# An LSTM's and an RNN's recurrent sums in two row blocks: twice the matmuls, half the PSUM columns

## The chip, the cores and the metric

One NeuronCore of a Trainium2 chip runs the kernel. The metric is the time of one execution on the device, in microseconds (us); lower is better.

## The reference, cut to what matters

Four sequences (`NB = 4`) of 1024 tokens with 512 features pass through four residual layers. Two of them are recurrent, and they set the order of everything:

```python
# layer 0, an RNN, 1024 steps
next_h = jnp.tanh(xw_t + prev_h @ Wh)                   # h: (4, 512), Wh: (512, 512)
# layer 1: a short convolution, projections, a state-space scan over the tokens
# layer 2, an LSTM, 1024 steps
A = xw_t + prev_h @ Wh                                  # Wh: (512, 2048)
i, f, o = sigmoid(A[:, 0:H]), sigmoid(A[:, H:2*H]), sigmoid(A[:, 2*H:3*H])
g = jnp.tanh(A[:, 3*H:4*H])
next_c = f * prev_c + i * g
next_h = o * jnp.tanh(next_c)
# layer 3: x @ (base_layer + a low-rank matrix of each sequence)
```

Each layer's result is added to its input.

## The kernel before, in words

**Chunks.** The tokens are cut into 32 chunks of 32 steps (`CT`). The layers run as a pipeline over chunks: while chunk i is in the RNN, chunk i-1 is in the state-space layer (`mid`), chunk i-2 in the LSTM and chunk i-3 in the output layer. So chunks 0 and 1 of the program have no LSTM, 2 to 31 have both recurrences, and 32 and 33 have the LSTM alone. Chunks 0 to 3 and 30 to 34 are written out; those between run in a hardware loop (`Fori`, line 246) whose pass holds two chunks. Within a chunk each engine's program goes through the 32 steps in a fixed order, written by hand; the other layers' work stands at certain steps (`SSM_STEP`, `L2_STEP` and others).

**One step on TensorE** (`products`, L968; the RNN's, L1007): first the LSTM's products of half 0 of the gates' columns, then of half 1, then the RNN's, then a few products of the other layers. h is the stationary operand, as two float16 parts: a high part in columns 0 to 3 and the rest in columns 16 to 19 of a tile of 20 (`LO + NB`), the columns between being zero. Wh, also in two float16 parts (`e`), streams. The output columns are spread over the four column tiles `j` of the array (`tile_position=(0, QC * j)`), so that tile j writes PSUM partitions 32j to 32j+19. For the LSTM a product is 128x20 by 128x256; a half has KB = 4 blocks `k`, two parts `e`, four tiles `j`: 32 products; the RNN's are 128x20 by 128x128, 32 of them. A half's first two blocks `k` need h of half 0 (`lstm_h_ready0`), the others h of half 1.

**One step on VectorE**, in order: transpose of the sums of half 0 (L754, 32x32 blocks, PSUM to `lstm_sums`), reduction (L760: the sum from the high part, that from the rest and the input part, which GpSimd has filled in at L344), transpose of half 1, product of gates 0 (L766), output gate (L775), reduction of half 1, new cell 0 (L771), the RNN's transpose (L815), products of gates 1, new h of half 0 (L783) and its two parts (L787, L791), which release TensorE's next step, the same for half 1, and last the RNN's reduction (L821) and the two parts of its h (L857, L859). ScalarE computes the tanh of the gates (L521), of the cell (L526) and of the RNN (L546) between them. GpSimd fills inputs (L344, L358) and runs the state-space layer's series (L371, L372) in certain steps.

**Preparation.** ScalarE converts the RNN's Wh to its high part (L478, four instructions) and VectorE subtracts to get the rest (L673, sixteen); the LSTM's Wh is split in chunk 0. The first step of each recurrence uses the float32 weights (L999, L943).

Of the kernel before, what the change touches and what calls it, by code (L numbers as in the profile page):

```python
# [7 lines left out]
F16 = mybir.dt.float16  # L8
# [6 lines left out]
P = 128  # L15
# [21 lines left out]
XS = 2 * LO  # L37
PIECES = [(0, 14), (14, 24), (24, 30), (30, 32)]
# [55 lines left out]
def resid_stack_kernel(nc, x, cond, l0_Wx, l0_Wh, l0_b, conv_b, Wp, bp, Ws, bs, A_log, dt_log, Wo, bo,  # L94
                       l2_Wx, l2_Wh, l2_b, base, w1, b1, w2, b2, ln_g, ln_b, out):
    ctx = ExitStack()
    with ctx:
# [33 lines left out]
        cond_r = sb("cond_rnn_scaled", [P, KB, LO + NB])  # L131
        cond_l = sb("cond_lstm_scaled", [P, KB, LO + NB])
# [36 lines left out]
        tr = [[sb(f"lstm_sums_{h}{e}", [P, HG, XS + NB]) for e in range(2)] for h in range(NH)]  # L169
# [66 lines left out]
        block = ctx.enter_context(nc.Block())  # L236

# [79 lines left out]
        def _(pool):  # L317
# [7 lines left out]
            def body(_i, par, known, w, p):  # L325
# [11 lines left out]
                def fill(s):  # L337

                    for h in range(NH):
                        if s >= 2:  # L340
                            pool.wait_ge(S[f"lstm_summed{h}"], s - 1)
                        elif p["lstm"]:
                            pool.wait_ge(S_last[f"lstm_summed{h}"], CT - 1 + s)
                        Q.tensor_copy(tr[h][s % 2][:, :, XS:XS + NB],  # L344
                                      xl[par][:, s, h * HG:(h + 1) * HG, :]).then_inc(S[f"lstm_in_ready{h}"], 1)

                def fill_rnn(s):
# [10 lines left out]
                    Q.tensor_copy(tr_r[s % 2][:, :, XS:XS + NB], xr[par][:, :, s, :]).then_inc(S["rnn_x_filled"], 1)  # L358
# [91 lines left out]
        def _(act):  # L450
# [41 lines left out]
            def body(_i, par, known, w, p):  # L492
# [14 lines left out]
                def lstm_weights(u):  # L507
# [7 lines left out]
                    for h in range(NH):  # L515
                        A.activation(whl[:, k, h, 0, :, g * HB * QC:(g + 1) * HB * QC].rearrange("p j (b c) -> p j b c", b=HB),
# [101 lines left out]
        def _(vec):  # L618
# [43 lines left out]
            prep(V.tensor_scalar(cond_r[:, :, 0:NB], condT, xscale_r[:, :], None, ALU.mult))  # L662
            V.tensor_scalar(b_rsc[:, :], b_rnn, xscale_r[:, :], None, ALU.mult).then_inc(r_scaled, 1)
            prep(V.tensor_scalar(cond_l[:, :, 0:NB], condT, 2 * H_SCALE, None, ALU.mult), wait=False)
# [3 lines left out]
            for k in range(KB):  # L668
                src = whr32[:, k, :].rearrange("p (b j c) -> p j b c", b=KB, c=QC)
                hi, lo = (whr[:, k, e, :, :].rearrange("p j (b c) -> p j b c", b=KB) for e in range(2))  # L670
# [66 lines left out]
            def body(_i, par, known, w, p):  # L737
# [48 lines left out]
                def hi_part(h, o3, t3):  # L786
                    return mark(V.tensor_tensor(half(hls, h)[:, :, 0:NB], o3, t3, ALU.mult))  # L787
# [358 lines left out]
```

## Time and profile before

| | |
|---|---|
| median of 3 runs | 4421.66 us (4418.98 to 4426.92) |
| profiled execution, its own time | 4419.02 us |
| its span in the profile | 4417.1 us |
| mean granted TensorE clock | 0.983 of full speed |
| TensorE, VectorE, ScalarE, GpSimd busy | 83%, 82%, 35%, 29% |
| TensorE matmuls, and as many weight loads | 106672 |

The span is that of the instructions; the execution's own time holds 1.9 us around it. Busy shares are means over stages with different limits. In the views PE is TensorE's matmuls, PEld its weight loads, DVE VectorE, ACT ScalarE, POOL GpSimd, SP SyncE; a name with a q (PEldq) is the sequencer of the engine. Ends of matmuls are modelled, and starts are recorded.

### The profile page before, as it was taken

To read this page: it belongs to the slowest core of one execution; us is meant where nothing else is said; L and a number is where in the kernel's file an instruction comes from. 1 tells how busy PE (TensorE), PEld (TensorE's weight loads), DVE (VectorE), ACT (ScalarE), POOL (GpSimd) and SP (SyncE) were. 2 spreads that over 40 slices of the span, in tenths; PEclk is the share of its full clock that TensorE was granted. 3 is DMA by queue.
4 is the path that set the end of the run, shared out by engine and by line. 5 is a ranking of instruction groups with operands and counts; after the bars stand their busy time and mean duration, and the time that the engine had idled before them with its cause. 6 is when DMAs were issued, how large, how long until landed. Compare 5 with 4: busy or idle time off the path is not lost.

```text
span 4417.1 us, 252254 instructions
## 1 busy us (share of the span) xinstructions
PE 3655.3 (83%) x106672; PEld 2960.4 (67%) x106672; DVE 3634.3 (82%) x20882; ACT 1559.4 (35%) x6724; POOL 1291.6 (29%) x4519
## 2 busy tenths in 40 slices
PE   7888888888888888888888888888888888888775
PEld 4566667676667676666676666777666767666653
DVE  5588888888888888888888888888888888888766
ACT  4233333333333333333333333333333333333321
POOL 0223332233332223333233333232333222333311
PEclk9899999999999999999999999999999999999999
DMA  7100000000000000000000000000000000000000
GB/s 247 42 4 9 9 6 8 8 6 8 8 6 8 8 6 8 8 8 6 8 9 6 8 8 6 9 8 6 8 8 6 9 8 6 8 6 4 6 5 7
DMA packets 18979, 62.51 MB, mean 14 GB/s; under 512 B 3942, under 2 KB 4510, under 8 KB 14834
## 3 DMA queue, kind: packets, MB, share of 16 engines
q1 hardware_dynamic: 17612, 46.54, 3.3%
q8 instruction: 836, 13.70, 1.3%
q14 instruction: 237, 1.94, 0.1%
q10 hardware_dynamic: 294, 0.33, 0.0%
HBM read 38.34 MB, written 8.39 MB: 11 GB/s over the span
## 4 chain that ended last, share of the span: by engine, by line
DVE 40%; PE 33%; ACT 11%; POOL 8%; issue 7%; SPq 1%; DMA 1%; DVEq 0%; ACTq 0%; POOLq 0%
PE ps_lstm L968 30%; DVE lstm_sums L754 11%; DVE lstm_arg L760 7%; DVE lstm_h_scaled L783 4%; ACT lstm_gates_2c L521 4%; ACT lstm_tanh_c L526 3%; DVE lstm_gates_2c L771 3%; POOL stage L371 3%; DVE lstm_ig_fc L766 2%; DVE lstm_h_parts L791 2%; POOL stage L372 2%; DVE rnn_h_parts L857 2%; DVE lstm_h_parts L787 2%; DVE lstm_o_scaled L775 2%; DVE rnn_arg L821 2%
## 5 line engine op out<-in xcount | busy, mean ns | idle before, releaser
L968 PE MATMUL ps_lstm<-lstm_Wh_parts,lstm_h_parts 128*20 128x256 f16 x65472 | 2027.8, 276 | 638.1 <-DVE lstm_h_parts L791 633.2
L968 PEld LDWEIGHTS ps_lstm<-lstm_Wh_parts,lstm_h_parts 128*20 128x20 f16 x65472 | 1508.0, 92 | 1146.6 <-DVE lstm_h_parts L791 945.3
L521 ACT ACTIVATE lstm_gates_2c<-lstm_arg 128x32 f32<-128x32 f32 x2048 | 469.8, 229 | 1624.7 <-DVE lstm_arg L760 1623.8
L754 DVE STREAM_TRANSPOSE lstm_sums<-ps_lstm 128x256 f32<-128x256 f32 x2048 | 912.1, 445 | 137.1 <-PE ps_lstm L968 86.9
L344 POOL COPY lstm_sums<-lstm_in 128x32 f32<-128x32 f32 x2048 | 417.8, 213 | 1368.2 <-DVE lstm_arg L760 1354.5
L1007 PE MATMUL ps_rnn<-rnn_Wh_parts,rnn_h_parts 128*20 128x128 f16 x32736 | 646.7, 221 | 46.2 <-DVE rnn_h_parts L859 46.1
L760 DVE TENSOR_REDUCE lstm_arg<-lstm_sums 128x32 f32<-128x96 f32 x2048 | 536.0, 262 | 120.9 <-DVE lstm_sums L754 19.6
L1007 PEld LDWEIGHTS ps_rnn<-rnn_Wh_parts,rnn_h_parts 128*20 128x20 f16 x32736 | 550.9, 93 | 99.1 <-DVE rnn_h_parts L859 82.7
L526 ACT ACTIVATE lstm_tanh_c<-lstm_gates_2c 128x8 f32<-128x8 f32 x2048 | 413.2, 202 | 394.3 <-DVE lstm_gates_2c L771 384.4
L546 ACT ACTIVATE rnn_h<-rnn_arg 128x16 f32<-128x16 f32 x1024 | 221.2, 216 | 771.0 <-DVE rnn_arg L821 771.0
L857 DVE TENSOR_SCALAR rnn_h_parts<-rnn_h 128x16 f16<-128x16 f32 x1024 | 240.0, 234 | 292.1 <-ACT rnn_h L546 292.1
L766 DVE SCALAR_TENSOR_TENSOR lstm_ig_fc<-lstm_gates_2c 128x16 f32<-128x16 f32 x2048 | 368.8, 180 | 31.4 <-ACT lstm_gates_2c L521 31.4
L791 DVE TENSOR_TENSOR lstm_h_parts<-lstm_h_scaled,lstm_h_parts 128x8 f16<-128x8 f32 x2048 | 356.9, 174 | 38.5 <-issue 2.0
L771 DVE SCALAR_TENSOR_TENSOR lstm_gates_2c<-lstm_ig_fc 128x8 f32<-128x8 f32 x2048 | 362.8, 177 | 6.8 <-DVE lstm_h_scaled L783 2.9
L783 DVE TENSOR_TENSOR lstm_h_scaled<-lstm_o_scaled,lstm_tanh_c 128x8 f32<-128x8 f32 x2048 | 343.7, 168 | 1.5 <-issue 0.3
L815 DVE STREAM_TRANSPOSE rnn_sums<-ps_rnn 128x128 f32<-128x128 f32 x1024 | 314.7, 307 | 35.7 <-PE ps_rnn L1007 35.1
L775 DVE TENSOR_SCALAR lstm_o_scaled<-lstm_gates_2c 128x8 f32<-128x8 f32 x2048 | 336.6, 164 | 0.0
L787 DVE TENSOR_TENSOR lstm_h_parts<-lstm_o_scaled,lstm_tanh_c 128x8 f16<-128x8 f32 x2048 | 327.6, 160 | 1.0 <-issue 0.9
L358 POOL COPY rnn_sums<-rnn_in 128x16 f32<-128x16 f32 x512 | 101.4, 198 | 675.8 <-DVE rnn_arg L821 604.0
L1083 PE MATMUL ps_lstm_in_a<-x,lstm_Wx 128*128 128x128 f32 x2048 | 298.5, 289 | 0.0
L358 POOL COPY rnn_sums<-stage 128x16 f32<-128x16 f32 x512 | 101.4, 198 | 671.9 <-DVE rnn_arg L821 598.5
L1083 PE MATMUL ps_lstm_in_b<-x,lstm_Wx 128*128 128x128 f32 x2048 | 296.5, 288 | 0.0
(176 smaller groups left out, 3390.3 us busy)
## 6 DMA issues: line engine op xcount, KB each, us to landing
layer_plus_2I<-in_L_cond_w SPq DMA_DIRECT2D x16, 1024.0 KB, 6.1
out<-out_rows SPq DMA_DIRECT2D x128, 64.0 KB, 1.9
x_rows<-in_x SPq DMA_DIRECT2D x31, 256.0 KB
lstm_Wx<-in_L_cond_Wh SPq DMA_DIRECT2D x1, 4096.0 KB, 19.2
lstm_Wx<-in_L_cond_Wx SPq DMA_DIRECT2D x1, 4096.0 KB, 14.2
layer_plus_2I<-in_L_cond_Wh SPq DMA_DIRECT2D x1, 1024.0 KB, 9.3
rnn_Wx<-in_L_cond_Wx SPq DMA_DIRECT2D x1, 1024.0 KB, 11.3
lstm_in<-in_L_cond_w SPq DMA_DIRECT2D x1, 1024.0 KB, 9.1
```

What stands on the lines that cost most here:

```text
L521: A.activation(gate[h][:, 0:G, :].rearrange("p g q -> p (g q)"), arg[h][:, :, :].rearrange("p g n -> p (g n)"), ACT.Tanh, scale=gate_scale ...
L526: A.activation(tc[h][:, :], cell[h], ACT.Tanh, scale=0.5).then_inc(S[f"lstm_tanhc{h}"], 1)
L754: return mark(V.transpose(tr[h][s % 2][:, :, 0:QC], psL[h][:, 0:HW].rearrange("p (g c) -> p g c", c=QC)))
L760: V.tensor_reduce(arg[h][:, :, :], three.rearrange("p g s n -> p g n s"), AX.X, ALU.add).then_inc(S[f"lstm_summed{h}"], 1)
L766: return mark(V.scalar_tensor_tensor(out=prod[h][:, :, :], in0=gate[h][:, 0:2, :], scalar=1.0, in1=gate[h][:, G - 1:G + 1, :], op0=ALU.add ...
L771: V.scalar_tensor_tensor(out=cell[h], in0=prod[h][:, 1, :], scalar=0.5, in1=prod[h][:, 0, :], op0=ALU.mult, op1=ALU.add).then_inc(S[f"lstm ...
L775: return mark(V.tensor_scalar(o_s[h][:, :], gate[h][:, 2, :], 1.0, H_SCALE, ALU.add, ALU.mult))
L783: at = mark(V.tensor_tensor(half(hl, h)[:, :, s, :], o3, t3, ALU.mult))
L791: V.tensor_tensor(half(hls, h)[:, :, LO:LO + NB], half(hl, h)[:, :, s, :], half(hls, h)[:, :, 0:NB], ALU.subtract).then_inc(S[f"lstm_h_rea ...
L968: ins = mm(psL[h][QC * j:QC * j + LO + NB, 0:HW], hls[:, k, :], whl[:, k, h, e, j, :], start=(k == 0 and e == 0), stop=(k == KB - 1 and e ...
L1007: last = mm(psR[QC * j:QC * j + LO + NB, 0:RW], hrs[:, k, :], whr[:, k, e, j, :], start=(k == 0 and e == 0), stop=(k == KB - 1 and e == 1) ...
L1083: last = mm((psA, psB)[g % 2][:, TOK * b:TOK * (b + 1)], w_, x2[:, k, :, :].rearrange("p t n -> p (t n)"), start=(k == 0), stop=(k == KB - 1))
```

## The change

The LSTM's sums of a half take two row blocks (`LB = 2`) in PSUM: the first half of the output columns goes to rows 0 to 3 of a tile, the second to rows 4 to 7, so the sums fill 128 columns instead of 256. For this the stationary tile is 24 columns wide (`LM`), and the tile in memory has four zero columns ahead (`LZ`): row block r reads it from column `LZ - NB*r`, so that h stands at columns 0 to 3 for r = 0 and 4 to 7 for r = 1, with zeros elsewhere, and both blocks add into the same rows. Each product of 256 columns becomes two of 128. The RNN's does the same with `RR = 2`: two products of 64 columns for one of 128. The transposes read half the columns; the reductions and GpSimd's fills have the same element counts with another order of axes; the weights' parts are stored in the order in which the products read them. In the preparation the RNN's conversions are cut in two, and its subtractions too. The core of the diff:

```diff
+LB = 2
+LQ = LB // HB
+LI = G // LQ
+LW = HW // LB
+LN = NB * LB
+RR = 2
+RI = KB // RR
+RN = NB * RR
+RZ = RN - NB
+RM = LO + RN
+RWR = RW // RR
+LZ = LN - NB
+LM = LO + LN
...
-        hrs = sb("rnn_h_parts", [P, KB, LO + NB], F16)
-        hls = sb("lstm_h_parts", [P, KB, LO + NB], F16)
-        tr_r = [sb(f"rnn_sums_{e}", [P, KB, XS + NB]) for e in range(2)]
+        hrs = sb("rnn_h_parts", [P, KB, RZ + RM], F16)
+        hls = sb("lstm_h_parts", [P, KB, LZ + LM], F16)
+        tr_r = [sb(f"rnn_sums_{e}", [P, RI, 3 * LO]) for e in range(2)]
...
-                        Q.tensor_copy(tr[h][s % 2][:, :, XS:XS + NB],
-                                      xl[par][:, s, h * HG:(h + 1) * HG, :]).then_inc(S[f"lstm_in_ready{h}"], 1)
+                        Q.tensor_copy(tr[h][s % 2][:, :, XS:XS + LN],
+                                      xl[par][:, s, h * HG:(h + 1) * HG, :].rearrange("p (i r) n -> p i (r n)", r=LB)).then_inc(S[f"lstm_in_ready{h}"], 1)
...
             for k in range(KB):
-                nc.scalar.activation(whr[:, k, 0, :, :].rearrange("p j (b c) -> p j b c", b=KB),
-                                     whr32[:, k, :].rearrange("p (b j c) -> p j b c", b=KB, c=QC),
-                                     ACT.Identity, scale=wscale[:, 0:1]).then_inc(r_hi, 1)
+                for q in range(RR):
+                    nc.scalar.activation(whr[:, k, 0, :, RWR * q:RWR * (q + 1)].rearrange("p j (i c) -> p j i c", c=QC),
+                                         whr32[:, k, :].rearrange("p (i q j c) -> p q j i c", q=RR, j=NQ, c=QC)[:, q],
+                                         ACT.Identity, scale=wscale[:, 0:1]).then_inc(r_hi, 1)
...
                 for j in range(NQ):
-                    ins = V.scalar_tensor_tensor(out=lo[:, j], in0=src[:, j], scalar=wscale[:, 0:1], in1=hi[:, j],
-                                                 op0=ALU.mult, op1=ALU.subtract)
+                    for i in range(RI):
+                        ins = V.scalar_tensor_tensor(out=lo[:, j, i], in0=src[:, j, i], scalar=wscale[:, 0:1], in1=hi[:, j, i],
+                                                     op0=ALU.mult, op1=ALU.subtract)
...
-                    return mark(V.transpose(tr[h][s % 2][:, :, 0:QC], psL[h][:, 0:HW].rearrange("p (g c) -> p g c", c=QC)))
+                    return mark(V.transpose(tr[h][s % 2][:, :, 0:QC], psL[h][:, 0:LW].rearrange("p (i c) -> p i c", c=QC)))
...
-                    V.tensor_reduce(arg[h][:, :, :], three.rearrange("p g s n -> p g n s"), AX.X, ALU.add
+                    three = tr[h][s % 2][:, :, :].rearrange("p i (s m) -> p i s m", m=LO)[:, :, :, 0:LN]
+                    V.tensor_reduce(arg[h][:, :, :].rearrange("p (i r) n -> p i (r n)", r=LB), three.rearrange("p i s m -> p i m s"), AX.X, ALU.add
...
-                    return mark(V.transpose(tr_r[s % 2][:, :, 0:QC], psR[:, 0:RW].rearrange("p (g c) -> p g c", c=QC)))
+                    return mark(V.transpose(tr_r[s % 2][:, :, 0:QC], psR[:, 0:RWR].rearrange("p (g c) -> p g c", c=QC)))
...
                             for e in parts:
-                                for j in range(NQ):
-                                    ins = mm(psL[h][QC * j:QC * j + LO + NB, 0:HW], hls[:, k, :], whl[:, k, h, e, j, :],
-                                             start=(k == 0 and e == 0), stop=(k == KB - 1 and e == 1), tile_position=(0, QC * j))
+                                for r in range(LB):
+                                    for j in range(NQ):
+                                        ins = mm(psL[h][QC * j:QC * j + LM, 0:LW], hls[:, k, LZ - NB * r:LZ - NB * r + LM],
+                                                 whl[:, k, h, e, j, LW * r:LW * (r + 1)], start=(k == 0 and e == 0 and r == 0),
+                                                 stop=(k == KB - 1 and e == 1 and r == LB - 1), tile_position=(0, QC * j))
...
                                 for e in range(2):
-                                    for j in range(NQ):
-                                        last = mm(psR[QC * j:QC * j + LO + NB, 0:RW], hrs[:, k, :], whr[:, k, e, j, :],
-                                                  start=(k == 0 and e == 0), stop=(k == KB - 1 and e == 1), tile_position=(0, QC * j))
+                                    for r in range(RR):
+                                        for j in range(NQ):
+                                            last = mm(psR[QC * j:QC * j + RM, 0:RWR], hrs[:, k, RZ - NB * r:RZ - NB * r + RM],
+                                                      whr[:, k, e, j, RWR * r:RWR * (r + 1)], start=(k == 0 and e == 0 and r == 0),
+                                                      stop=(k == KB - 1 and e == 1 and r == RR - 1), tile_position=(0, QC * j))
```

## Rows read from the trace of the kernel before

**Rows 1.** Page: busy us, share and instructions; the chain by engine.

```profile
PE 3655.3 (83%) x106672; PEld 2960.4 (67%) x106672; DVE 3634.3 (82%) x20882; ACT 1559.4 (35%) x6724; POOL 1291.6 (29%) x4519
...
DVE 40%; PE 33%; ACT 11%; POOL 8%; issue 7%; SPq 1%; DMA 1%; DVEq 0%; ACTq 0%; POOLq 0%
```

**Rows 2.** Chain in order of time, a steady step: start us, us, what.

```profile
2102.22 0.45 DVE lstm_sums L754
...
2104.04 1.96 PE ps_lstm L968 x64
...
2106.02 0.45 DVE lstm_sums L754
```

**Rows 3.** The same chain, in the steps with the state-space layer.

```profile
2067.56 3.11 PE ps_lstm L968 x64
...
2084.84 0.22 DVE rnn_arg L821
...
2096.24 0.53 DVE stage L806 x2
```

**Rows 4.** Page, groups: count, busy us, mean ns of one, idle before.

```profile
L968 PE MATMUL ps_lstm<-lstm_Wh_parts,lstm_h_parts 128*20 128x256 f16 x65472 | 2027.8, 276 | 638.1 <-DVE lstm_h_parts L791 633.2
...
L754 DVE STREAM_TRANSPOSE lstm_sums<-ps_lstm 128x256 f32<-128x256 f32 x2048 | 912.1, 445 | 137.1 <-PE ps_lstm L968 86.9
...
L1007 PE MATMUL ps_rnn<-rnn_Wh_parts,rnn_h_parts 128*20 128x128 f16 x32736 | 646.7, 221 | 46.2 <-DVE rnn_h_parts L859 46.1
...
L815 DVE STREAM_TRANSPOSE rnn_sums<-ps_rnn 128x128 f32<-128x128 f32 x1024 | 314.7, 307 | 35.7 <-PE ps_rnn L1007 35.1
```

**Rows 5.** Timeline of that steady step: start us, us, instructions.

```profile
2104.04 1.93 PE L968 MATMUL ps_lstm<-lstm_Wh_parts,lstm_h_parts 128*20 128x256 f16 x64 [0.31 <-DVE lstm_h_parts L791]
2105.80 0.62 PE L1007 MATMUL ps_rnn<-rnn_Wh_parts,rnn_h_parts 128*20 128x128 f16 x32
...
2106.02 0.45 DVE L754 STREAM_TRANSPOSE lstm_sums<-ps_lstm 128x256 f32<-128x256 f32 x1
...
2106.83 0.31 DVE L815 STREAM_TRANSPOSE rnn_sums<-ps_rnn 128x128 f32<-128x128 f32 x1
```

**Rows 6.** Groups by form, 10 to 24 us (preparation).

```profile
L673 DVE SCALAR_TENSOR_TENSOR rnn_Wh_parts<-layer_plus_2I,wscale,rnn_Wh_parts 128x128 f16<-128x128 f32 x16 | 4.3, 333 | 0.0
...
L478 ACT ACTIVATE rnn_Wh_parts<-layer_plus_2I,wscale 128x512 f16<-128x512 f32 x4 | 2.6, 710 | 2.2 <-DVE rnn_in_scale L660 2.2
```

**Rows 7.** Page, DMA queues, whole span: packets, MB, share of 16 engines.

```profile
q8 instruction: 836, 13.70, 1.3%
```

**Rows 8.** DMA queues in one pass of the loop, 2043.3 to 2305.8 us.

```profile
q8 instruction: 52, 0.85, 1.4%
```

**Rows 9.** Windows: us, busy (instructions) per engine, TensorE clock, DMA, GB/s.

```profile
2043.30:2305.80 262.50, 222.13 (x6613) 181.82 (x6604) 222.65 (x1295) 94.52 (x415) 80.58 (x282) 0.99 0.03 8
2070.68:2074.75 4.07, 4.07 (x139) 3.42 (x135) 3.52 (x21) 0.98 (x5) 0.62 (x3) 0.91 0.01 4
...
4300.00:4400.00 100.00, 53.89 (x1642) 39.08 (x1646) 68.45 (x409) 19.88 (x103) 11.65 (x52) 0.97 0.02 5
```

**Rows 10.** The loop's line: ns min/median/max, first and last start.

```profile
L246 PEldq COMPARE_BRANCH  x14: 88/352/387, 464.8 to 3883.5; - x14
```

**Rows 11.** Timeline of TensorE behind the loop's last branch.

```profile
3885.02 0.39 PE L968 MATMUL ps_lstm<-lstm_Wh_parts,lstm_h_parts 128*20 128x256 f16 x5 [0.56 <-DVE lstm_h_parts L791]
3887.18 3.12 PE L968 MATMUL ps_lstm<-lstm_Wh_parts,lstm_h_parts 128*20 128x256 f16 x56 [1.77 <-issue]
```

**Rows 12.** DMA, 3884.4 to 3886.0 us; the digits are 40 equal slices.

```profile
DMA  0009000000000000000000000000000000000000
...
q8 instruction: 1, 0.02, 5.0%
```

**Rows 13.** DMA, 3888.2 to 3889.0 us.

```profile
DMA  0000900000000000000000000000000000000000
```

**Rows 14.** Line of the LSTM's transpose: ns, first and last start, forms.

```profile
L754 DVE STREAM_TRANSPOSE lstm_sums<-ps_lstm x2048: 377/450/452, 203.4 to 4405.3; 128x256 f32<-128x256 f32 x187
```

More of the change, by code:

```diff
@@ L163, in resid_stack_kernel @@
         orow = sb("out_rows", [P, D])
-        hrs = sb("rnn_h_parts", [P, KB, LO + NB], F16)
-        hls = sb("lstm_h_parts", [P, KB, LO + NB], F16)
-        tr_r = [sb(f"rnn_sums_{e}", [P, KB, XS + NB]) for e in range(2)]
+        hrs = sb("rnn_h_parts", [P, KB, RZ + RM], F16)
+        hls = sb("lstm_h_parts", [P, KB, LZ + LM], F16)
+        tr_r = [sb(f"rnn_sums_{e}", [P, RI, 3 * LO]) for e in range(2)]
         arg_r = sb("rnn_arg", [P, KB, NB])
-        tr = [[sb(f"lstm_sums_{h}{e}", [P, HG, XS + NB]) for e in range(2)] for h in range(NH)]
+        tr = [[sb(f"lstm_sums_{h}{e}", [P, HG // LB, 3 * LO]) for e in range(2)] for h in range(NH)]
         arg = [sb(f"lstm_arg{h}", [P, HG, NB]) for h in range(NH)]
@@ L939, in prepare @@
                     pe.wait_ge(l_src, G * (k + 1))
-                    w5 = whl32[:, k, :].rearrange("p (g h b j c) -> p h j g b c", g=G, h=NH, b=HB, j=NQ)
+                    w6 = whl32[:, k, :].rearrange("p (i q h b j c) -> p h j q b i c", q=LQ, h=NH, b=HB, j=NQ, c=QC)
                     for h in range(NH):
-                        for j in range(NQ):
-                            last = mm(psL[h][QC * j:QC * j + LO + NB, 0:HW], cond_l[:, k, :], w5[:, h, j],
-                                      start=(k == 0), stop=(k == KB - 1), tile_position=(0, QC * j))
+                        for r in range(LB):
+                            for j in range(NQ):
+                                last = mm(psL[h][QC * j:QC * j + LM, 0:LW], cond_l[:, k, LZ - NB * r:LZ - NB * r + LM],
+                                          w6[:, h, j, r // HB, r % HB], start=(k == 0 and r == 0),
+                                          stop=(k == KB - 1 and r == LB - 1), tile_position=(0, QC * j))
                     last.then_inc(lstm_h0_mm, 1)
@@ L996, in body @@
                             for k in range(KB):
-                                for j in range(NQ):
-                                    w_ = whr32[:, k, :].rearrange("p (b j c) -> p j b c", b=KB, c=QC)[:, j]
-                                    last = mm(psR[QC * j:QC * j + LO + NB, 0:RW], cond_r[:, k, :], w_,
-                                              start=(k == 0), stop=(k == KB - 1), tile_position=(0, QC * j))
+                                for r in range(RR):
+                                    for j in range(NQ):
+                                        w_ = whr32[:, k, :].rearrange("p (i q j c) -> p q j i c", q=RR, j=NQ, c=QC)[:, r, j]
+                                        last = mm(psR[QC * j:QC * j + RM, 0:RWR], cond_r[:, k, RZ - NB * r:RZ - NB * r + RM], w_,
+                                                  start=(k == 0 and r == 0), stop=(k == KB - 1 and r == RR - 1),
+                                                  tile_position=(0, QC * j))
                             last.then_inc(rnn_h0_mm, 1)
```

40 lines of the change are left out of this document (22 added, 18 removed).

## The prediction

> **What bounds the kernel now.** I read the busy line of the page first: TensorE is busy 83% of the span and VectorE 82%, and the chain that ended last gives 40% to VectorE and 33% to TensorE [rows 1]. Neither is saturated; they take turns in a recurrence. So the chain in a steady stretch comes next [rows 2]. It repeats every 3.80 us (2102.22 to 2106.02): transpose of the second half's sums 0.45, then reduction, tanh of the gates, cell and h of the first half, and 1.96 in which TensorE makes all 64 products of the next step. The half that ends last on TensorE starts the next transpose. 1024 LSTM steps of 3.80 would be 3891; the rest is the two first chunks and steps in which the state-space part holds things up. One of these holds is GpSimd's series, from 2084.84 to 2096.24, in which three steps pass [rows 3]: nothing done to the LSTM chain shortens that stretch.
>
> **What the products cost.** The groups give 276 ns for one 256-column product and 221 for one of 128 [rows 4]. Four products, one per column tile, run side by side. The LSTM's 64 take 1.93 from the first start to the last end, the RNN's 32 take 0.62 [rows 5]. So a group of four comes every (1.93 - 0.28) / 15 = 0.110 us with 256 columns and every (0.62 - 0.23) / 7 = 0.056 with 128: about 0.42 ns a column and 2 ns more.
>
> **The change on the chain.** LSTM: 64 products of 256 columns become 128 of 128, in 32 groups: 31 x 0.056 + 0.23 = 1.97 instead of 1.93, +0.04. The loads go from 20 to 24 columns; they are issued during the group before and are covered by it, as the RNN's 20-column loads are at this same pace. The transposes of the LSTM sums go from 128x256 (445 ns) to 128x128, which the RNN's transpose shows at 307 [rows 4]: -0.14 each, and one of the two lies on the chain; the other is on VectorE's own round, which is shorter than 3.80. The reductions keep their element counts (96 in, 32 out; 48 in, 16 out), GpSimd's fills too, so they stay what and where they are. Step: 3.80 + 0.04 - 0.14 = 3.70.
>
> RNN: 32 products of 128 become 64 of 64, in 16 groups. Nothing of 64 columns and four tiles is in the trace. Below, the column slope gives 0.029 a group, the same 0.46 in all as now; above, 0.056, which 128 columns take, 0.90 in all. I take 0.029, since the loads are short and everything here has followed the columns. The RNN's transpose is due 0.81 after the LSTM's second one (2106.02 and 2106.83) [rows 5], 0.67 after the change. With 0.029 its sums are there 0.47 after; with 0.056 at 0.87, and the 0.2 that it is late delays what VectorE has queued behind it (products of half 1, new h of half 0), so the step is back at about 3.80. Its own transpose falls by about 64 x 1.08 ns = 0.07, hidden behind ScalarE's tanh of the gates except in the two RNN-only chunks.
>
> Preparation: four conversions of 710 ns become eight of half the size, sixteen VectorE subtractions of 333 become thirty-two [rows 6]. I put +2 us on it, 0 to 4. The first f32 products and the split of the LSTM weights move the same elements.
>
> **What the change adds off the chain: instructions.** Every product is a load and a multiply. TensorE runs 2 x 106672 instructions now [rows 1]. A step gains 2 x 64 for the LSTM and 2 x 32 for the RNN. They have to be fetched. The instruction queue q8 moved 836 packets, 13.70 MB [rows 7]: 16.4 KB and 255 TensorE instructions a packet, so this queue is TensorE's, and nothing is kept between passes of the loop: one pass of two chunks (262.5 us) shows 52 packets for its 6613 + 6604 records [rows 8, 9]. That is a block of 256 instructions every 5.05 us. After the change a pass has 64 x 192 = 12288 more, 48 blocks, 100 in all: one every 2.63 us if the time stayed.
>
> How fast can they come? The only place where the trace shows TensorE out of instructions is the end of the loop. Its last branch is at 3883.5 and takes 88 ns [rows 10]. The LSTM burst starts at 3885.02, stops after 5 matmuls, and goes on at 3887.18; the wait is put down to "issue", 1.77, not to another engine [rows 11]. Between, there is one q8 packet: it starts at 3884.52 to 3884.56 (fourth slice of 0.04) and is busy 5.0% of 16 engines in 1.6 us, 1.28 us [rows 12]. The next one starts at 3888.28 to 3888.30 [rows 13], 1.1 after TensorE went on. I read: the block that would follow had not been fetched, the branch (here not taken) asked for it, the packet began 1.0 later and the instructions could be used 3.63 after the request; passing into that block asked for the next. One packet at the miss and one at the crossing, not a run of several, says that the fetch is one block ahead and no more. The mean packet is shorter, 0.013 x 16 x 4417 / 836 = 1.10. So from crossing to use: 1.0 + 1.10 + 1.37 = 3.45 us. Today that is hidden: the densest stretch that I found, 4.07 us, holds 139 + 135 records [rows 9], about a block, and is longer than 3.45. It is not much longer, and after the change a block lasts 2.4 us at a step of 3.70 (400 instructions a step, 1.56 blocks).
>
> The Trainium skill ("Runtime: NRT & Kernel Launch", section "Instruction fetch mechanics") speaks of 16 KiB blocks of 256 instructions, which the q8 rows agree with; of 128 KiB for TensorE, eight such blocks; and of a fetch that is hidden since the sequencer issues more slowly than the blocks arrive. By that the change gets its gain, the second case below. The stop after the loop, with one packet in it, is against the last part here.
>
> **The sum.** A block takes 3.45, so a pass of 100 takes 345 instead of 262.5: +82.5. Fifteen pairs of chunks (2 to 31) run LSTM and RNN together: +1238. The gains of the chain vanish, for it waits. The two RNN-only chunks (the LSTM's first transpose is at 203.4 [rows 14]) have some 19 blocks each, 66 us, in 90 or more: nothing. The two LSTM-only chunks have 34, 117 us, in 32 x 3.80 = 122 or more: nothing. Preparation +2. The profiled execution's own time is 4419.0 (span 4417.1, 1.9 around it), 2.6 under the median: 4419 + 1238 + 2 = **5660**.
>
> **Rivals.**
> (a) *The fetch keeps up, the change does what it says.* For it: no stall anywhere inside the loop, and a block store larger than two blocks could hide everything; the one stop might be the price of a wrong guess at a branch alone. Then 29 of 32 steps gain 0.11 (3.70, and 0.14 in the few where TensorE is done early), 30 chunks: -96, the LSTM-only chunks -6, the RNN-only ones -4, +2: about 4315.
> (b) *A prefetched block can be used as soon as its packet ends*, 1.0 + 1.10 = 2.1 after the crossing. On average that suffices (1.56 x 2.1 = 3.3 a step), but a block that begins in the first half of the LSTM burst is used up in 1.4 to 1.8 us and stalls 0.3 to 0.7 in the RNN's products. It decides at 2.63 us a block: below, 4330 to 4450; above, 1500 us for each us.
> (c) *The 64-column groups take 0.056* with fetch in time: about 4420, no change.
> (d) *The stalls let the clock fall.* TensorE would be busy some 60% of the time; a stretch at 54% shows 0.97 of the full clock [rows 9], so I expect little; at the lower of its two levels (1.2 instead of 2.4 GHz) the columns take twice as long. A burst that fell partly in such a stretch took 3.11 instead of 1.96 [rows 3]. All bursts at that level: 32 x 0.107 = 3.4 us, 1.5 more, the RNN's and the other products 0.7 more on the chain, so a step of some 5.9, and 30 chunks of 189 instead of 131: 6150.
>
> The Trainium skill ("TensorE: Matmul & The Clock Gate", section "Wait — 56ns, not 53.3ns?") gives a floor of about 25 ns from start to start of matmuls, however small. The RNN's 32 come at 14 ns each [rows 5], so for four column tiles the row disagrees; by the floor the LSTM's 128 would take 3.2 us and the step 4.9.
>
> **How the numbers follow.** Fetch-bound at 3.2 to 3.7 us a block: 64%, 5280 to 6030. Fetch-bound between 2.65 and 3.2: 7%, 4450 to 5280. (d): 4%. (a): 20%. (b) below its point and (c): 5%, 4410 to 4450 mostly, which I count as the same. A time within 0.2% could hardly be told from no change. Faster 20%, same 4%, slower 76%. The range leaves (a) out and takes the rest: 4410 to 6050; that of the likeliest case alone is 5280 to 6030.
>
> **What would show it.** Right: q8 near 1600 packets with the spacing of a block never under some 3.4 us; TensorE idle with "issue" ahead of L1007 or in the middle of L968's burst; VectorE far under 82%; transposes of about 0.31 and 0.24; LSTM bursts of 1.97 where they aren't cut. Wrong: steps of 3.70 with 100 packets a pass. The step that decides is the reading of one stop as the latency of every block.

## The result and the profile after

The changed kernel takes **5971.15 us** (median of 4 runs, 5969.11 to 5972.12); the kernel before, beside it, 4423.97 (4 runs, 4418.98 to 4426.92). The ratio is 1.3498, with a 95% interval of 1.3475 to 1.3522: 35% slower. Forecast were 5660, with 5280 to 6030 for the likeliest case.

The page of the kernel after, the lines that answer to [rows 1], [rows 4] and [rows 7]:

```profile
PE 4194.4 (70%) x204976; PEld 3622.3 (61%) x204976; DVE 3300.1 (55%) x20898; ACT 1560.9 (26%) x6728; POOL 1292.1 (22%) x4519
...
q8 instruction: 1604, 26.28, 1.8%
...
PE 55%; issue 27%; DVE 12%; ACT 4%; POOL 1%; DMA 0%; DVEq 0%; SPq 0%; POOLq 0%
...
L991 PE MATMUL ps_lstm<-lstm_Wh_parts,lstm_h_parts 128*24 128x128 f16 x130944 | 2381.9, 230 | 737.9 <-issue 538.7
```

Two numbers tell the story before any detail. Both engines that took turns are less busy (TensorE 83 to 70%, VectorE 82 to 55%), so neither has become the bound; and 27% of the chain is "issue", time in which TensorE waited for nothing that the profile shows. Before, the LSTM's products waited for VectorE's h, 633.2 of 638.1 us [rows 4]; now most of their idle time is "issue".

Next the timeline of TensorE in two ordinary steps of the kernel after (start us, us, instructions, idle before and its cause):

```profile
3000.82 1.22 PE L991 MATMUL ps_lstm<-lstm_Wh_parts,lstm_h_parts 128*24 128x128 f16 x66
3002.53 1.07 PE L991 MATMUL ps_lstm<-lstm_Wh_parts,lstm_h_parts 128*24 128x128 f16 x62 [0.49 <-issue]
3003.38 0.74 PE L1034 MATMUL ps_rnn<-rnn_Wh_parts,rnn_h_parts 128*24 128x64 f16 x64
3004.05 0.49 PE L1129 MATMUL ps_lstm_in_a<-xT,rnn_Wx 128*128 128x128 f32 x2
3006.30 1.34 PE L1129 MATMUL ps_lstm_in_a<-xT,rnn_Wx 128*128 128x128 f32 x6 [1.77 <-issue]
```

The line to read is the count. Between the two stops stand 62 + 64 + 2 = 128 products, each a load and a multiply: 256 instructions, whatever line they are from. The stop falls in the middle of a burst, once behind the LSTM's product 66, once behind two f32 products of the input layer. The instruction queue in 3003.6 to 3005.2 us of the kernel after (40 equal slices of 0.04):

```profile
DMA  0000000000900000000000000000000000000000
...
q8 instruction: 1, 0.02, 3.7%
```

One packet, starting at 3004.00, long 3.7% of 16 engines in 1.6 us, 0.95 us, so ended at 3004.95; TensorE goes on 1.35 later, at 3006.30. Between 1000 and 3500 us TensorE stops 564 times with "issue", 685.6 us in all; the kernel before has no such stop there. The median from the packet's end to the next instruction is 1.40 us, and the next packet starts 1.15 us after that. The count holds widely: of the 1002 intervals from one such stop to the next between 600 and 5100 us, 780 hold 128 products, and most others 256 or 384, where a block ended without a stop.

Where the 1551.8 us of span (4417.1 to 5968.9) lie follows from the first start of the LSTM's transpose and its starts at the borders of the chunks. Of the kernel after (ns, first and last start; before, [rows 14]):

```profile
L774 DVE STREAM_TRANSPOSE lstm_sums<-ps_lstm x2048: 244/317/319, 215.0 to 5957.2; 128x128 f32<-128x128 f32 x187
```

The two RNN-only chunks end at 215.0 instead of 203.4, +11.6. The 30 chunks with LSTM and RNN take 5493.3 instead of 3948.4, +1544.9. The two LSTM-only chunks take 127.8 and 132.9 instead of 130.9 and 134.4, -4.6. So nearly all of it is in the pairs of chunks, 366.2 us instead of 263.2, and one such pair (2956.6 to 3323.5) shows 100 q8 packets, as counted ahead.

### The profile page after: what moved, and what is told of

It is laid out like the page before. It is cut to its first block, busy times and chain, and to the rows that moved or that the text cites. A ratio compares the mean times of both kernels' runs of the same rounds, so it can differ in the third digit from the quotient of the medians.

```text
span 5968.9 us, 448882 instructions
## 1 busy us (share of the span) xinstructions
PE 4194.4 (70%) x204976; PEld 3622.3 (61%) x204976; DVE 3300.1 (55%) x20898; ACT 1560.9 (26%) x6728; POOL 1292.1 (22%) x4519
## 4 chain that ended last, share of the span: by engine, by line
PE 55%; issue 27%; DVE 12%; ACT 4%; POOL 1%; DMA 0%; DVEq 0%; SPq 0%; POOLq 0%
PE ps_lstm L991 38%; PE ps_rnn L1034 7%; PE ps_lstm_in_a L1111 3%; DVE lstm_sums L774 2%; PE ps_lstm_in_b L1111 2%; DVE lstm_arg L780 2%; ACT lstm_gates_2c L540 2%; PE ps_lstm_in_a L1129 2%; DVE lstm_h_scaled L803 2%; DVE lstm_h_parts L811 1%; PE ps_ssm L1072 1%; DVE lstm_gates_2c L791 1%; ACT lstm_tanh_c L545 1%; DVE lstm_h_parts L807 1%; DVE lstm_o_scaled L795 1%
## 5 line engine op out<-in xcount | busy, mean ns | idle before, releaser
L991 PE MATMUL ps_lstm<-lstm_Wh_parts,lstm_h_parts 128*24 128x128 f16 x130944 | 2381.9, 230 | 737.9 <-issue 538.7
L991 PEld LDWEIGHTS ps_lstm<-lstm_Wh_parts,lstm_h_parts 128*24 128x24 f16 x130944 | 2053.9, 99 | 1129.1 <-issue 691.1
L1034 PE MATMUL ps_rnn<-rnn_Wh_parts,rnn_h_parts 128*24 128x64 f16 x65472 | 823.2, 196 | 944.3 <-issue 914.7
L1034 PEld LDWEIGHTS ps_rnn<-rnn_Wh_parts,rnn_h_parts 128*24 128x24 f16 x65472 | 698.6, 93 | 1018.9 <-issue 966.2
L774 DVE STREAM_TRANSPOSE lstm_sums<-ps_lstm 128x128 f32<-128x128 f32 x2048 | 647.0, 316 | 1185.7 <-PE ps_lstm L991 1173.6
L835 DVE STREAM_TRANSPOSE rnn_sums<-ps_rnn 128x64 f32<-128x64 f32 x1024 | 252.4, 246 | 897.9 <-PE ps_rnn L1034 897.6
L791 DVE SCALAR_TENSOR_TENSOR lstm_gates_2c<-lstm_ig_fc 128x8 f32<-128x8 f32 x2048 | 349.4, 171 | 5.2 <-issue 0.3
L786 DVE SCALAR_TENSOR_TENSOR lstm_ig_fc<-lstm_gates_2c 128x16 f32<-128x16 f32 x2048 | 314.1, 153 | 42.2 <-ACT lstm_gates_2c L540 13.8
L1111 PE MATMUL ps_lstm_in_a<-x,lstm_Wx 128*128 128x128 f32 x2048 | 316.0, 299 | 26.4 <-issue 26.4
L1111 PE MATMUL ps_lstm_in_b<-x,lstm_Wx 128*128 128x128 f32 x2048 | 308.5, 296 | 0.8 <-issue 0.8
```

Of the source, the lines that this page charges most:

```text
L774: return mark(V.transpose(tr[h][s % 2][:, :, 0:QC], psL[h][:, 0:LW].rearrange("p (i c) -> p i c", c=QC)))
L791: V.scalar_tensor_tensor(out=cell[h], in0=prod[h][:, 1, :], scalar=0.5, in1=prod[h][:, 0, :], op0=ALU.mult, op1=ALU.add).then_inc(S[f"lstm ...
L991: ins = mm(psL[h][QC * j:QC * j + LM, 0:LW], hls[:, k, LZ - NB * r:LZ - NB * r + LM], whl[:, k, h, e, j, LW * r:LW * (r + 1)], start=(k == ...
L1034: last = mm(psR[QC * j:QC * j + RM, 0:RWR], hrs[:, k, RZ - NB * r:RZ - NB * r + RM], whr[:, k, e, j, RWR * r:RWR * (r + 1)], start=(k == 0 ...
L1111: last = mm((psA, psB)[g % 2][:, TOK * b:TOK * (b + 1)], w_, x2[:, k, :, :].rearrange("p t n -> p (t n)"), start=(k == 0), stop=(k == KB - 1))
```

## The experiments

Each kernel ran beside the kernel before on the same chip; where no interval is given, it ran once.

### Is it the number of instructions?

**The LSTM's part alone.**

```diff
-RR = 2
+RR = 1
```

> The changed kernel with the RNN put back (one row block of 128 columns). Theory F, the fetch: TensorE's instructions come in blocks of 256 and a new block takes 3.65 us, whatever is in it (the changed kernel's loop pass of two chunks: 364.8 us, 100 blocks). Here a pass has 52 + 32 = 84 blocks, 307 us instead of 262.5, for 15 such pairs of chunks: about 5085 us, q8 near 1350 packets. Rival P, the products: the LSTM's smaller products are what costs (they are two thirds of the added products and lie on the chain, the RNN's do not): then nearly all of the 1550 us stays, 5800 to 5970. Rival R, the 64-column products of the RNN cost: the time falls to about 4320.

Measured: 5071.3 us, 1348 q8 packets. The 30 chunks took 4607.1, 307.1 a pair for 84 blocks: 3.66 us each, the same price as in the kernel after. The rest of the loss came with the RNN's part, which isn't on the chain: against the products as such.

**The kernel before with 64 small products a step more.**

```diff
+                        if known is None:
+                            extra(64)
+            def extra(n):
+                for u in range(n):
+                    a = QC * (2 + u % 2)
+                    mm(psS[a:a + NB, 3 * TOK:3 * TOK + NB], whr[:, 0, 0, 0, 0:NB], whr[:, 0, 0, 0, 0:NB],
+                       start=True, stop=True, tile_position=(0, a))
```

> The kernel before, its sums, transposes and products untouched, with 64 more products a step inside the loop (26 of 35 chunks): 4 columns each, 4 rows out, into an unused part of PSUM, in two column tiles, behind the RNN's products of the step, where TensorE has 1.4 us to spare. Nothing reads them. Theory F: 52 + 32 = 84 blocks a pass, 307 us instead of 262.5, 13 passes: about 5000 us, and TensorE stops inside its LSTM bursts. Rival P (what costs is the LSTM and RNN products in their smaller form, not their number of instructions): TensorE's added time is 64 x 14 to 25 ns = 0.9 to 1.6 us a step, mostly hidden: 4420 to 4650.

Measured: 5060.6 us, 1252 packets. Nothing of the LSTM, the RNN or the transposes has changed here, and yet the timeline of this kernel has the same stops inside its 256-column bursts:

```profile
2060.87 0.83 PE L975 MATMUL ps_lstm<-lstm_Wh_parts,lstm_h_parts 128*20 128x256 f16 x22
2062.40 1.37 PE L975 MATMUL ps_lstm<-lstm_Wh_parts,lstm_h_parts 128*20 128x256 f16 x42 [0.70 <-issue]
2063.50 0.72 PE L1014 MATMUL ps_rnn<-rnn_Wh_parts,rnn_h_parts 128*20 128x128 f16 x32
2064.04 0.83 PE L883 MATMUL ps_ssm<-rnn_Wh_parts 128*4 128x4 f16 x54
2065.90 0.27 PE L883 MATMUL ps_ssm<-rnn_Wh_parts 128*4 128x4 f16 x10 [1.02 <-issue]
```

Again 42 + 32 + 54 = 128 products from stop to stop. But the added products, some 0.9 us a step, don't fit beside the second layer's input products, so this time holds two causes. A control took them apart: **16 products of 128 columns in one column tile at the same place**, the same 0.9 us of TensorE in a quarter of the instructions.

```diff
-                            extra(64)
+                            extra(16)
-                    a = QC * (2 + u % 2)
-                    mm(psS[a:a + NB, 3 * TOK:3 * TOK + NB], whr[:, 0, 0, 0, 0:NB], whr[:, 0, 0, 0, 0:NB],
+                    a = QC * 2
+                    mm(psS[a:a + NB, 3 * TOK:4 * TOK], whr[:, 0, 0, 0, 0:NB], whr[:, 0, 0, 0, 0:P],
```

> Control for the kernel before with 64 small products a step (5061 us; they took 0.88 us of TensorE a step, more than it has free in the steps with the second layer's input products). Here 16 products of 128 columns stand in one column tile, one behind the other, at the same place: 16 x 0.056 = 0.90 us of TensorE, but 32 instructions instead of 128, 60 blocks a pass instead of 84. Theory F: only TensorE's time is added, 0.45 + 0.90 + 1.1 + 1.93 = 4.3 to 4.4 instead of 3.80 in some 17 of 32 steps, 26 chunks: 4450 to 4680. If TensorE's time was what counted in the other, this one is as slow: 5060.

Measured: 4601.1 us. It is 176 over the kernel before beside it (4424.7), the one with 64 small products 638 (4423.0). TensorE's time accounts for the 176, in a kernel that has no stop with "issue" between 1000 and 3500 us; the other 461 go with the 96 instructions that a step has more.

**The kernel after with half of its columns streamed**, so that half of the sums are left out.

```diff
-mm(psL[h][QC * j:QC * j + LM, 0:LW], hls[...], whl[:, k, h, e, j, LW * r:LW * (r + 1)], ...)
+mm(psL[h][QC * j:QC * j + LM, 0:LW // 2], hls[...], whl[:, k, h, e, j, LW * r:LW * r + LW // 2], ...)
-mm(psR[QC * j:QC * j + RM, 0:RWR], hrs[...], whr[:, k, e, j, RWR * r:RWR * (r + 1)], ...)
+mm(psR[QC * j:QC * j + RM, 0:RWR // 2], hrs[...], whr[:, k, e, j, RWR * r:RWR * r + RWR // 2], ...)
```

> The changed kernel, but each product of the loop over steps streams half of its columns (64 instead of 128 for the LSTM, 32 instead of 64 for the RNN), so that half of the sums are left out; the number of instructions is the same. Theory F: 100 blocks at 3.65 us a pass as in the changed kernel, no change: 5900 to 5975 us. Rival P (time goes with what TensorE streams): the LSTM burst falls by 31 x 0.027 = 0.8 us a step and the RNN's by up to 0.2: 0.8 x 960 = 770 us less, about 5200.

Measured: 5947.8 us, 23 less than the kernel after, where by the expectation's rival streaming half would have saved 770. It also bears on the clock. Here is the windows view of four kernels over the same 2500 us of the loop (window, its length, busy us and instructions of TensorE, its loads, VectorE, ScalarE, GpSimd; granted clock, DMA share, GB/s). The kernel before:

```profile
1000.00:3500.00 2500.00, 2110.52 (x63191) 1732.48 (x63182) 2123.39 (x12330) 907.37 (x3959) 767.07 (x2684) 0.99 0.03 8
```

The kernel after:

```profile
1000.00:3500.00 2500.00, 1750.12 (x87075) 1526.23 (x87074) 1375.67 (x8829) 647.15 (x2826) 541.41 (x1905) 0.95 0.03 8
```

The kernel after with half of its columns:

```profile
1000.00:3500.00 2500.00, 1643.96 (x87631) 1406.49 (x87613) 1374.84 (x8875) 655.39 (x2842) 550.59 (x1925) 0.79 0.03 8
```

The LSTM's part alone:

```profile
1000.00:3500.00 2500.00, 1944.15 (x87451) 1651.64 (x87438) 1695.06 (x10562) 776.31 (x3389) 658.44 (x2308) 0.99 0.03 8
```

Read the counts in brackets. Three kernels with different work, at granted clocks of 0.95, 0.79 and 0.99, run 87075, 87631 and 87451 products in 2500 us: 35 a microsecond, 256 instructions every 3.65 to 3.68 us. The kernel with 64 products more has 86391. The kernel before runs 63191, bound by something else. The price of a block doesn't go with the clock: at 0.79 it is no higher than at 0.99. In the kernel after itself, the LSTM burst at 3007.57 took 3.14 instead of 1.97 us, at a granted clock of 0.58; yet the 256 products from 3006.30 to the next stop's end at 3013.58 took 7.28 us, 3.64 a block.

### What a block costs by itself, and what is kept

**TensorE alone**: the output is a copy of x and nothing of the kernel is computed. Six stretches of 1536 products are written out, then come loops over 64-column products.

```python
for u in range(1536):
    mm(ps[QC * (u % NQ):QC * (u % NQ) + 20, 0:4], wt[:, 0:20], mv[:, 0:4], start=True, stop=True, tile_position=(0, QC * (u % NQ)))
...
with nc.Fori(0, 84, 1, ...) as i:
    for u in range(60):
        mm(ps[QC * (u % NQ):QC * (u % NQ) + 20, 0:64], wt[:, 0:20], mv[:, 0:64], start=True, stop=True, tile_position=(0, QC * (u % NQ)))
```

> TensorE alone, nothing else of the kernel (the output is a copy of x). Six stretches written out, 1536 products (3072 instructions, 12 blocks) each: column tiles with 4, 64, 128 columns, then whole-array products of 64, 128, 256 columns. Then loops over 64-column products in column tiles whose bodies are 120, 504, 1016, 1528, 1784, 2040, 2552 instructions long, some 5100 products in each. Theory F: the first three stretches take the same, 12 x 3.5 to 3.65 = 42 to 44 us each, however few the columns; whole-array products of 256 columns (128 of them are over 13 us) hide the fetch, and those of 128 (6.9 us for 128 of them) do too. Rival P: the three stretches go with their columns, 14 ns a product for 128 and less for 64 and 4, 22 us and below. The loops: if nothing is kept but the block in use and the next one, every body of 1016 and more instructions fetches on every pass, as the kernel's loop does; if eight blocks are kept, bodies up to about 1784 fetch once only and then run at the products' own pace.

The lines view of that kernel (L91, L93, L95: column tiles with 4, 64, 128 columns; L97, L99: whole array, 64 and 128 columns; L104: the loop of 120 instructions, L122 that of 2552):

```profile
L99 PE MATMUL sums<-moving,weights 128*128 128x128 f16 x1536 | 85.9, 219 | 0.0
L122 PE MATMUL sums<-moving,weights 128*20 128x64 f16 x3828 | 55.9, 240 | 52.9 <-issue 52.9
L104 PE MATMUL sums<-moving,weights 128*20 128x64 f16 x5040 | 53.8, 194 | 21.7 <-issue 21.7
L97 PE MATMUL sums<-moving,weights 128*128 128x64 f16 x1536 | 45.3, 193 | 0.3 <-issue 0.2
...
L95 PE MATMUL sums<-moving,weights 128*20 128x128 f16 x1536 | 25.2, 225 | 18.2 <-issue 18.2
L93 PE MATMUL sums<-moving,weights 128*20 128x64 f16 x1536 | 22.9, 241 | 19.8 <-issue 19.8
L91 PE MATMUL sums<-moving,weights 128*20 128x4 f16 x1536 | 14.0, 171 | 36.8 <-issue 34.9 <-DVE sums L72 1.8
```

Busy and idle together give the three straight stretches in column tiles 49.0 (without the 1.8 of waiting for the start, with three dearer first blocks), 42.7 and 43.4 us for 12 blocks: 64 and 128 columns cost the same. From the timeline of this kernel, the stretch with 4 columns:

```profile
28.60 1.17 PE L91 MATMUL sums<-moving,weights 128*20 128x4 f16 x128 [2.29 <-issue]
32.05 1.17 PE L91 MATMUL sums<-moving,weights 128*20 128x4 f16 x128 [2.29 <-issue]
35.78 1.17 PE L91 MATMUL sums<-moving,weights 128*20 128x4 f16 x128 [2.56 <-issue]
```

and the one with 64, in the same view:

```profile
53.87 1.89 PE L93 MATMUL sums<-moving,weights 128*20 128x64 f16 x128 [1.78 <-issue]
57.60 1.89 PE L93 MATMUL sums<-moving,weights 128*20 128x64 f16 x128 [1.84 <-issue]
61.05 1.89 PE L93 MATMUL sums<-moving,weights 128*20 128x64 f16 x128 [1.56 <-issue]
```

128 products each, and 3.45 or 3.73 us from start to start; two of the later intervals of the stretches in column tiles are 4.00. A block of 4-column products is done in 1.17 us, one of 64 in 1.89, and the next comes at the same time after its predecessor *began*: in both, the packet starts 1.1 us behind the first instruction of a block. So the request for the next block goes out when a block is entered, not when it is used up. The first three blocks are an exception: they took 6.63, 6.20 and 6.74 us. During them the copy of x (8192 KB, 23.2 us to landing) was under way, and their packets start 3.7 to 4.3 us behind the first instruction, while lasting 0.92 to 0.98 as ever. So a busy DMA may hold the request back; no run varied that alone. Nor does the fetch run further ahead when it has time: through the whole-array stretches of 128 and 256 columns (7.1 and 14.0 us a block, no stop) the packets come one a block, in step with the instructions, and the blocks of the loops behind them, which a longer lead would have brought by then, were still fetched on entering each loop.

The loops show what is kept. Packets on q8 in the time of each loop: body of 120 instructions none, 504 one, 1016 four, 1528 six, 1784 seven, 2040 eight. These are the blocks of the body, fetched once, for 4 to 19 rounds. The same 64-column products that wait in the straight stretch run faster there. The loop of 504 instructions by its line (ns, first and last start):

```profile
L107 PE MATMUL sums<-moving,weights x4788: 190/195/199, 511.4 to 560.3; 128*20 128x64 f16 x200
```

That is 48.9 us for 4788, 10.2 ns each, against 42.7 us for 1536, 27.8 each, where every block is fetched. So 27.8 is not what TensorE needs to take an instruction; it is the arrival. The body of 2552, ten blocks, had this in its window (788.5 to 897 us):

```profile
q8 instruction: 31, 0.51, 1.8%
```

ten for each of its three rounds and one, at 3.5 us a block again, and this at a granted clock of 0.51 (791 to 896 us). A body of eight blocks stays, and one of ten is fetched afresh on every pass; none of nine was run. By the Trainium skill ("Runtime: NRT & Kernel Launch", section "Instruction fetch mechanics") TensorE's store is 128 KiB, eight blocks of 16 KiB; these loops agree. By the same section the fetch is mostly hidden; here it is not.

### What the change is worth when fetch is out of the way

**Half 1 of the LSTM alone in two row blocks**, the half whose transpose lies on the chain; and **the RNN's part alone**. In both the constants of the LSTM are per half:

```diff
-LB = 2
...
-LW = HW // LB
...
+LBS = (1, 2)          # the RNN's part alone: (1, 1), with RR = 2
+LWS = [HW // b for b in LBS]
...
-RR = 2               # half 1 alone
+RR = 1
```

> Only half 1 of the LSTM in two row blocks of 128 columns (the half whose transpose lies on the chain), half 0 and the RNN as before: 52 + 16 = 68 blocks a pass. Theory F: 68 x 3.6 = 245 us is under the 262.5 of a pass, so the mean is no longer the bound; but a light step then has some 265 instructions, 3.7 to 3.8 us of fetch, and steps with the second layer's input products 280 to 290, 4.0, against 3.80 now; what the held-up steps lose can't be made up, since only one block is fetched ahead. So between 4390 and 4520, 4440 likeliest: the chain's gain of 0.11 a step is mostly eaten. If several blocks were fetched ahead, the mean would count: 4320.

> Only the RNN's part of the change (64 columns in two row blocks), the LSTM as before: again 68 blocks a pass, but none of the gain on the chain. Theory F: like the one with half 1 alone, plus 0.11 a step where fetch doesn't bind: 4430 to 4550. A rival by which it is the LSTM's smaller products that cost: 4420, no change. If 64-column groups took 0.056 us as 128-column ones do: 4420 to 4500 too, but then the RNN's burst shows it, 0.9 us instead of 0.5 to 0.6 from first to last.

Measured: half 1 alone 4478.6 (ratio 1.0097, interval 1.0070 to 1.0124); the RNN's part alone 4506.9 (1.0177, 1.0150 to 1.0204). Both are slower at 68 blocks a pass, though 68 x 3.65 = 248 us would fit into the 263 of a pass. In 2500 us of the loop they had 635 and 631 packets, one every 3.9 to 4.0 us, near the price of a block, and TensorE stopped with "issue" 165 and 166 times, 83.7 and 82.5 us in all. So the mean is not the rule; what is lost in a dense stretch is not made up in a thin one. The RNN's 64-column products themselves are as fast as taken: 0.70 us from the first start to the last end where uncut.

**The same with the RNN's low parts left out**, with the kernel before treated likewise as base (44 blocks a pass), so that fetch has room:

```diff
-                                for e in range(2):
+                                for e in range(1):
```

> The kernel before with half of the RNN's products left out (those with the low parts of its weights), so that a pass has 44 blocks. It is the base of the next one. The RNN isn't on the chain, so 4400 to 4420 in any theory.

> Half 1 of the LSTM in two row blocks, and the same half of the RNN's products left out: 44 + 16 = 60 blocks a pass, 219 us of fetch in 262.5, 3.4 us a step in 3.80. Here the fetch should bind (almost) nowhere, so the difference to the kernel before with the same products left out is what the narrower transpose is worth by itself: step 3.80 to 3.70 (-0.14 for the transpose, +0.02 to 0.04 for the burst), 29 of 32 steps, 30 chunks: 90 to 105 us less, about 4315. If the gain isn't real even so, no difference.

> The same as the kernel with half 1 in two row blocks and the low half of the RNN's products left out (4369), but with half 0 in two row blocks in place of half 1: 60 blocks a pass, fetch out of the way again. The prediction counted one of the two transposes only, since half 1's lies on the chain and half 0's on VectorE's own round. If so, this one is where its base is, 4415 to 4430, or a little above for TensorE's 0.04 a step. If VectorE's whole order is what counts, it gains like half 1: 4370.

Measured: base 4424.5, half 1 4369.2, half 0 4421.6. Between 1000 and 3500 us none of the three stops with "issue", so fetch is out of the way. Half 1's narrower transpose is worth 55 us, half 0's nothing that one run can tell (runs of the kernel before lay 4418 to 4435; beside the first two it took 4428.9, beside half 0, on another chip, 4431.8). The LSTM's transposes in the kernel with half 1 changed, groups by form:

```profile
L774 DVE STREAM_TRANSPOSE lstm_sums<-ps_lstm 128x256 f32<-128x256 f32 x1024 | 456.1, 445 | 108.3 <-PE ps_lstm L992 101.0 <-issue 6.6
L774 DVE STREAM_TRANSPOSE lstm_sums<-ps_lstm 128x128 f32<-128x128 f32 x1024 | 319.2, 312 | 73.6 <-PE ps_lstm L992 18.9
```

The two kinds differ by 445 - 312 = 133 ns, 0.14 forecast. From one transpose of half 0 to the next, the median step went from 3.80 to 3.73, the faster quarter to 3.69; with half 0 changed it is 3.82. The gain of the change is real, but 55 and not the 90 to 105 reckoned. The steps of the loop's 26 chunks show where the rest is. Of the 32 steps of a chunk 20 got shorter by 0.08 to 0.14, 2.1 us together, where 29 steps with 0.11, 3.2, had been counted. The fifth got 0.6 longer and the thirteenth 0.2, and in these two TensorE's granted clock was 0.81 and 0.90 on average, instead of 0.91 and 0.94 in the base. With half 0 changed the fifth step was at 0.95 and 0.3 shorter. So the totals hold such shifts too, and the light steps, 0.11 shorter with half 1 changed and 0.02 longer with half 0, are the cleaner measure. That the clock is what moves those two steps fits, but no run held it fixed.

**An attempt to have both.** The RNN's products with the high and the low weights share their h, so they can be one product of 256 columns; that takes 8 blocks out of a pass, and half 1's row blocks put 16 in.

```diff
-                                for e in range(2):
-                                    for r in range(RR):
-                                        for j in range(NQ):
-                                            last = mm(psR[QC * j:QC * j + RM, 0:RWR], hrs[...], whr[:, k, e, j, ...], ...)
+                                for j in range(NQ):
+                                    last = mm(psR[QC * j:QC * j + RM, 0:2 * RW], hrs[:, k, :],
+                                              whr[:, k, :, j, :].rearrange("p e (g c) -> p g e c", c=QC), ...)
-V.transpose(tr_r[s % 2][:, :, 0:QC], psR[:, 0:RWR].rearrange("p (g c) -> p g c", c=QC))
+V.transpose(tr_r[s % 2][:, :, 0:2 * QC], psR[:, 0:2 * RW].rearrange("p (g c) -> p g c", c=2 * QC))
```

> A kernel meant to keep the transpose's gain and stay under the fetch. Half 1 of the LSTM in two row blocks (+16 blocks a pass), and the RNN's products with the high and the low part of its weights, which have the same h, made as one of 256 columns instead of two of 128: 16 instead of 32 a step (-8 blocks), their sums side by side; the transpose of the RNN's sums grows from 128x128 to 128x256 and its reduction from three terms to five. 60 blocks a pass, 3.4 us of fetch a step, as in the kernel with the RNN's low parts left out, which was 55 us under its base. Theory F: that gain less what the longer transpose (+0.14) and reduction (+0.05 to 0.1) of the RNN cost where VectorE is behind: 4370 to 4440, 4400 likeliest. If the fetch weren't the cause of half 1's loss (4479), this kernel would be as slow as that one or slower, 4480 to 4550.

> The kernel before with only the RNN's products merged as in the one above: 44 blocks a pass. It shows what the merging costs by itself. Before isn't bound by fetch, so nothing is gained by fewer instructions; the longer transpose and reduction on VectorE lie partly on the chain: 4420 to 4500, 4440 likeliest.

Measured: with half 1, 4425.3 (ratio 1.0001, interval 0.9992 to 1.0010): no difference from before. The merging by itself, 4488.0 (1.0143, 1.0128 to 1.0159), more than the 4440 held likeliest. So on top of the merged RNN half 1 saves 63 us, and against half 1 alone the merging saves 53 by leaving fetch room (no stop with "issue" between 1000 and 3500 us); but by itself it costs 63, with longer work on VectorE. The page of the kernel with both:

```profile
L835 DVE STREAM_TRANSPOSE rnn_sums<-ps_rnn 128x256 f32<-128x256 f32 x1024 | 451.3, 441 | 33.2 <-PE ps_rnn L1033 32.4
...
L841 DVE TENSOR_REDUCE rnn_arg<-rnn_sums 128x16 f32<-128x80 f32 x1024 | 291.2, 284 | 7.9 <-POOL rnn_sums L375 1.1
```

and its chain, by engine:

```profile
DVE 53%; ACT 16%; PE 12%; issue 9%; POOL 8%; DVEq 0%; DMA 0%; SPq 0%; POOLq 0%; ACTq 0%
```

The RNN's transpose is 441 ns instead of 307, and TensorE's share of the chain has fallen to 12%: VectorE, at 53% of the chain instead of 40%, is now most of what bounds it. No kernel tried here that makes the whole result is faster than the one before.

## Why the prediction was right, and where its numbers were off

- **The bound, and that it would change**: right. The change adds 48 blocks of 256 instructions to a pass, and TensorE's instructions then arrive more slowly than it can use them. The 100 packets a pass, the stops with "issue" inside L991's burst and ahead of L1034, VectorE at 55%, and the products that count alike whatever they stream, all show it.
- **One stop read as the latency of every block**, the step named as the one that decides: right. The request goes out on entering a block, one block ahead. With TensorE alone a block took mostly 3.45 or 3.73 us, in the kernel 3.66; read were 3.45 (the three terms as written, 1.0 + 1.10 + 1.37, add up to 3.47). The part from the packet's end to the first instruction measured 1.40 (1.37 taken), the packet 1.09 (1.10), from the first instruction to the packet 1.15 (1.0). This term is the one that was mis-sized: (3.66 - 3.45) x 100 x 15 = 315 us, of a miss of 311. That one stop gave a price so near is in part luck: single blocks in the loop range from 3.49 to 4.05 (5% and 95% of those between two stops).
- **A sign that wasn't met word for word**: "never under some 3.4 us". Between 1000 and 3500 us the median from packet to packet is 3.64, but some 5% of the spacings are under 3.39, the shortest 2.98.
- **"Nothing is kept between passes"**: right for this loop only because its 52 blocks are more than 8. As a statement on the chip it would be wrong.
- **The RNN-only chunks, "nothing"**: wrong by a little, +11.6 up to the LSTM's first transpose, instead of the +2 of the preparation. Their means fit, their dense stretches don't: the first of them has 7 stops, 9.6 us, ahead of the RNN's products. The kernels bear it out: where the RNN's part is in, the LSTM starts at 214.4 or 215.0; with the LSTM's part alone at 207.6, so some 4 of the 11.6 aren't the RNN's.
- **The LSTM-only chunks**: -4.6 where "nothing" was put into the sum.
- **The LSTM burst**: 1.97 us forecast, 1.97 measured where uncut and at the full clock. Transposes 0.317 and 0.246 (0.31 and 0.24 forecast). The 64-column groups of the RNN follow the columns: (0.70 - 0.20) / 15 = 0.033 us a group, near the lower bound of 0.029 that was taken, so rival (c) falls.
- **Rival (a)**, its size: with fetch out of the way half 1's transpose gave 55 us, not 90 to 105. Light steps fell by 0.08 to 0.14 as reckoned, but they are 20 of 32 and not 29; the heavy ones, held by other work, did not, and two of them got longer at a lower granted clock.
- **Rival (b)**, a block usable at its packet's end: falls, 1.40 us lie between.
- **Rival (d)**, the clock: it did fall somewhat, 0.99 to 0.95, and cost nothing that can be seen: at 0.79 the kernel with half of the columns was 23 us faster than the one at 0.95. Full columns at the lower level throughout, the 6150 of this rival, weren't tried. That 6150 also lies outside the range of 4410 to 6050, which is said to leave only (a) out.

## What to carry to other kernels

Count instructions as a resource of their own: packets on the instruction queue per pass of the loop, times the time that a block takes, against the time of the pass; and count them in the densest step too, since a lead of one block can't carry a surplus over. An edit that halves what each instruction does and doubles their number is safe only where that count has room, or where the loop fits into what the engine keeps. "Issue" in the middle of a burst, with the same number of instructions from stop to stop across different lines, is the mark of it. Judge a small gain by the light steps and not by the total alone: here a few steps at a lower clock may have hidden part of it.

## What the runs showed of the hardware

- A block of 256 TensorE instructions takes 3.45 to 3.73 us to come in most cases, whatever is in it and at either clock level: 27 to 29 ns for each load and multiply. While a copy of 8192 KB was under way, three blocks took 6.2 to 6.7 us. Products in four column tiles can be issued much faster, (1.17 - 0.17) / 127 = 7.9 ns from start to start with 4 columns and (0.70 - 0.20) / 63 = 7.9 with 64, so such code is bound by its fetch unless its bursts are short or its blocks are kept (10.2 ns each in the loop of 504 instructions).
- With whole-array products of 128 columns (55.8 ns each, 85.7 us for 1536) a block lasts 7.1 us and the fetch can't be seen; with 64 columns (29.6 ns each, 45.4 us for 1536) 3.8 us, and it is just hidden.
- The fetch leads by one block even though eight blocks are kept: loops of up to 2040 instructions ran from what is kept, one of 2552 did not.
- The stops don't need a long queue of work to hurt: at a mean of 3.9 to 4.0 us a block, over the 3.65 of the fetch, the two kernels with 68 blocks a pass were already 1.0 and 1.8% slower; with 60 none stopped between 1000 and 3500 us.
